# The reciprocal square root of the key norms moved from VectorE to GpSimd in a fused decoder layer

## What is computed

```python
q = jax.nn.elu(q) + 1.0
k = jax.nn.elu(k) + 1.0
k = k / jnp.sqrt(jnp.sum(k * k, axis=-1, keepdims=True) + EPS)    # EPS = 1e-6, over the 8 numbers of a head
scores = jnp.einsum('bhqd,bhkd->bhqk', q, k)
attn = jnp.einsum('bhqk,bhkd->bhqd', scores, v)
```

## Time and profile before

| | us |
|---|---|
| time, median of 2 runs | 458.34 |
| the two runs | 457.92 and 458.75 |
| span of the profiled execution | 457.6 |
| VectorE (DVE) busy | 384.1 |
| TensorE (PE) busy | 378.9 |
| GpSimd (POOL) busy | 296.1 |
| ScalarE (ACT) busy | 251.1 |

### The profile page before, as it was taken

The page is one execution under the profiler, slowest core; times in us unless marked ns, Lnnn a source line. Parts: engine busy times, 40 slices in busy tenths (PEclk is TensorE's granted clock), DMA queues, the critical chain, the costliest instruction groups (busy, mean ns, idle before and its releaser), DMA issues. The chain is left out here.

```text
span 457.6 us, 8365 instructions
## 1 busy us (share of the span) xinstructions
PE 378.9 (83%) x2057; PEld 263.5 (58%) x2057; DVE 384.1 (84%) x953; ACT 251.1 (55%) x483; POOL 296.1 (65%) x464
## 2 busy tenths in 40 slices
PE   3998878899898979898898989797989888977562
PEld 3776547657474746566565747484837475637242
DVE  2678885699999999999999989999999996956562
ACT  2646265565655555656565656666556554634232
POOL 1014586787777777787786858686867778554123
PEclk9999999999999999999999989999989998998756
DMA  8500000000000000000000000000000000000000
GB/s 235 107 13 1 13 1 13 7 6 11 3 12 13 11 11 0 23 0 23 0 23 0 23 0 23 0 23 0 23 0 23 0 12 2 11 2 11 1 11 23
DMA packets 13683, 8.20 MB, mean 18 GB/s; under 512 B 992, under 2 KB 13280, under 8 KB 13664
## 3 DMA queue, kind: packets, MB, share of 16 engines
q1 hardware_dynamic: 13376, 6.93, 5.6%
q10 hardware_dynamic: 288, 1.05, 0.7%
HBM read 5.88 MB, written 2.10 MB: 17 GB/s over the span
## 5 line engine op out<-in xcount | busy, mean ns | idle before, releaser
L1534 PE MATMUL S<-M,x1T 128*128 (+1 forms) x128 | 60.8, 597 | 0.0
L1574 PE MATMUL F<-w_gu,wT 128*128 128x352 f32 x128 | 48.5, 503 | 7.4 <-DVE h L1127 3.5
L472 POOL TENSOR_TENSOR xo_w<-pe 128x512 f32<-128x512 f32 x32 | 42.8, 1337 | 4.2 <-ACT pe L760 4.1
L1082 DVE TENSOR_REDUCE smax<-S 128x16 fp32r<-128x1024 f32 x32 | 39.1, 1221 | 5.4 <-DVE stats_post_attn L1049 2.8
L760 ACT ACTIVATE pe<-S 128x1024 f32<-128x1024 f32 x32 | 32.5, 1015 | 19.5 <-PE S L1542 19.5
L1542 PE MATMUL S<-smax,ident_r 128*128 128x512 f32 x64 | 24.0, 458 | 22.8 <-DVE smax L1082 22.7
L1574 PEld LDWEIGHTS F<-w_gu,wT 128*128 128x128 f32 x128 | 22.7, 197 | 33.5 <-DVE h L1127 14.0
L497 POOL TENSOR_TENSOR wT<-wT,hs 128x704 f32<-128x704 f32 x16 | 22.2, 1386 | 28.0 <-DVE wT L939 28.0
L460 POOL TENSOR_TENSOR kn<-fk,krn 128x256 f32<-128x256 f32 x16 | 11.1, 692 | 42.2 <-DVE krn L1038 42.2
L481 POOL TENSOR_TENSOR fw_v<-pe,srec 128x1024 f32<-128x1024 f32 x16 | 30.4, 1902 | 11.6 <-DVE srec L1094 11.6
L1524 PE MATMUL TP<-HW,ctx_cur 128*64 128x512 f32 x128 | 34.2, 660 | 0.0
(11 more groups left out here) (179 smaller groups left out, 1038.6 us busy)
## 6 DMA issues: line engine op xcount, KB each, us to landing
x_sb<-in_x SPq DMA_DIRECT2D x16, 128.0 KB, 2.1
out<-xv_w SPq DMA_DIRECT2D x16, 128.0 KB, 1.8
xk_w<-in_L_xattn_Wk ACTq DMA_DIRECT2D x1, 512.0 KB, 4.0
ctx_rows<-in_ctx SPq DMA_DIRECT2D x1, 512.0 KB, 6.9
xv_w<-in_L_xattn_Wv ACTq DMA_DIRECT2D x1, 512.0 KB, 6.6
xq_w<-in_L_xattn_Wq SPq DMA_DIRECT2D x1, 512.0 KB, 7.7
xo_w<-in_L_xattn_Wo SPq DMA_DIRECT2D x1, 512.0 KB, 9.4
fw<-in_L_ffn_w_gate SPq DMA_DIRECT2D x3, 64.0 KB, 4.2
```

What stands on the lines that cost most here:

```text
L472: ge.tensor_tensor(phalf[t].rearrange("p (h r) -> p h r", h=HX), p4[:, :, 0, :], p4[:, :, 1, :], ALU.add).then_inc(fold_made, 1)
L1082: ve.tensor_reduce(smax[:, t, :], S[:, :].rearrange("p (h r) -> p h r", h=HX), AX.X, ALU.max, negate=True).then_inc(smax_made, 1)
L1534: last = te.matmul(S[:, half * BANK:half * BANK + BANK], x1T[:, t * P:t * P + P], M[:, HC * half:HC * half + HC, bass.ds(b * R, R)], start ...
L1574: last = te.matmul(bk[:, 0:I], xfT[:, t * P:t * P + P], w_gu[:, m, :], start=True, stop=True)
```

## The change

The addition and the reciprocal square root become two instructions of GpSimd, ahead of k_norm: kse = kss + eps_attn, and krn = kse to the power neg_half, both on 128x32. The eleven operations leave VectorE. krn_step counts two steps per batch instead of eleven, and the tiles kyy and kxyy go.

```diff
@@ gpsimd
+            def k_rsqrt(b):
+                pool.wait_ge(kss_made, b + 1)
+                if late(b):
+                    pool.wait_ge(krn_step, 2 * b)
+                ge.tensor_tensor(kse[:, :], kss[:, :], eps_attn[:, :], ALU.add).then_inc(krn_step, 1)
+                pool.wait_ge(krn_step, 2 * b + 1)
+                if late(b):
+                    pool.wait_ge(kn_made, b)
+                ge.tensor_tensor(krn[:, :], kse[:, :], neg_half[:, :], ALU.pow).then_inc(krn_step, 1)
+
             def k_norm(b):
-                pool.wait_ge(krn_step, 11 * b + 11)
+                pool.wait_ge(krn_step, 2 * b + 2)
...
                 if b0 is not None:
+                    k_rsqrt(b0)
                     k_norm(b0)
@@ vector
             def k_sums(b):
                 dve.wait_ge(ksq_made, b + 1)
                 if late(b):
-                    dve.wait_ge(krn_step, 11 * b)
+                    dve.wait_ge(krn_step, 2 * b)
...
-            def k_rsqrt(b, first, last):
-                for k in range(first, last):
-                    if k:
-                        dve.wait_ge(krn_step, 11 * b + k)
-                    else:
-                        dve.wait_ge(kss_made, b + 1)
-                    if k == 0:
-                        ve.tensor_scalar(kse[:, :], kss[:, :], ATTN_EPS, None, ALU.add).then_inc(krn_step, 1)
-                    elif k == 1:
...
             def iteration(i):
                 b0, b1, b2, b3, b4, b5 = (on(i, n) for n in range(6))
-                if b1 is not None:
-                    k_rsqrt(b1, 4, 5)
...
-                    k_rsqrt(b1, 10, 11)
                 keep_units(i, {1: (11,)})
...
-                if b0 is not None:
-                    k_rsqrt(b0, 0, 1)
```

More of the change, by code:

```diff
@@ L58, in decoder_layer @@
     STEP = 2.0 ** 22
-    RSQRT_MAGIC = float(0x5F3759DF)
     HIGH_MASK = -(1 << 12)
@@ L130, in decoder_layer @@
         krn = sb("krn", [P, T * HA])
-        kyy = sb("kyy", [P, T * HA])
-        kxyy = sb("kxyy", [P, T * HA])
         kn = sb("kn", [P, T, P])
@@ L1259, in iteration @@
                     aggregate("ffn", b5)
-                if b0 is not None:
-                    k_rsqrt(b0, 0, 1)
                 keep_units(i, {0: (5,), 1: (25,)})
-                if b0 is not None:
-                    k_rsqrt(b0, 1, 2)
                 keep_units(i, {0: (7,)})
@@ L1268, in iteration @@
                 keep_units(i, {0: (9,)})
-                if b0 is not None:
-                    k_rsqrt(b0, 2, 3)
                 if b4 is not None:
                     gate_times(b4, 0)
-                if b0 is not None:
-                    k_rsqrt(b0, 3, 4)
                 if b4 is not None:
```

## The result

The changed kernel takes **541.74 us** (median of 2 runs, 540.59 to 542.88), the kernel before 458.34 us. The ratio is 1.181, with a 95% interval of 1.176 to 1.187: slower by 18%. The forecast was 558 us, with 478 to 596 as its range.

The account below looks back on a forecast made before the run. The prediction took the ring from kss through kvT to the next kss as the bound, not VectorE's busy time. 458.3 + 92.4 for the turns + 7.2 for the clock gave 558 us, range 478 to 596.

Parts of the forecast that it names:

- The ring: Path every turn goes round once, kss to kvT and on to the next kss: 23.65 us, setting the turn.
- The way from kss to kvT = 5.46 + X: From kss's end to kvT's start via GpSimd's addition, power and kn: 5.46 us plus X, against 6.79 before.
- X: Time of GpSimd's power on 128x32, forecast 7.5 us; break-even at 1.33, each microsecond moving the whole by 16 us.
- I put a tenth of it there: Pricing the power: 0.05 of the 499 ns by which it exceeds an addition is paid once, the rest by column.
- The clock: TensorE's granted clock falls in every steady turn after 7 us standing: 0.9 us in eight previously spared turns, 7.2 us.
- The sum: Eleven steady turns at 6.17 us, 67.9, plus the first five turns: 92.4 us; with the clock's 7.2, 557.9 us.
- GpSimd busy should rise by 124 us: Expected sign: GpSimd's added power and addition, 7.75 us in each of 16 turns, raise its busy time.
- VectorE's fall by up to 45: Expected sign: VectorE's busy time falls by up to 45 us as its eleven instructions leave.
- Columns partly overlapped: Rival: the power's column arithmetic overlaps, X 1.9 to 5 us; 491 us at X = 3.3, span 468 to 518; 27 in 100.
- A fixed amount: Rival: the power's extra cost is paid once per instruction, X 0.75 us; 449 us, span 448 to 467; 12 in 100.
- The clock stays down: Rival: standing keeps TensorE at 1.2 GHz all the turn, making it the bound; about 670 us; 3 in 100.
- has just room: GpSimd's queue from kvT on, with kn ending 0.8 us and not 1.7 us before kvT; no cost was added.

## Why the prediction was right, and where it was off

**The ring, not the busy time, decides: right.** The eleven instructions are gone from VectorE and the kernel is 18% slower. The power twice gave 15.7 us per us of power, against 16 forecast. Downwards, with half the columns, it was 22; that the clock's loss shrank with it is the likely reason and was not tried.

**The way from kss to kvT = 5.46 + X: right, with 0.2 us too little.** In the run with ten filling products, where the clock stays up over this stretch, kss ends at 250.99 and kvT starts at 262.14:

```profile
250.60 0.39 DVE L1022 TENSOR_REDUCE kss<-ksq 128x32 f32<-128x256 f32 x1
...
262.14 0.29 DVE L1029 TENSOR_TENSOR kvT<-A,head_mask 128x128 f32<-128x128 f32 x1 [5.01 <-PE A L1463]
...
278.82 0.39 DVE L1022 TENSOR_REDUCE kss<-ksq 128x32 f32<-128x256 f32 x1
```

That is 11.15 us, and 5.46 + 5.44 = 10.90. From kvT to the end of the next kss it is 17.07, against 16.85. Together 0.47 us more in a turn than the sum says. Of this, 0.19 stand ahead of the addition: it starts 3.79 us after the end of kss, not 3.60, and a small power ahead of it takes 0.98 us, where the row of before has 0.73.

```profile
251.03 0.98 POOL L518 TENSOR_TENSOR rstd_post_attn<-veps_post_attn,neg_half 128x2 f32<-128x2 f32 x1
```

Why it does, and where the rest falls, was not tried.

**X, the size of the power: off by 2.06 us (7.5 against 5.44).** The step that failed is "I put a tenth of it there": of the 499 ns by which a power on two columns exceeds an addition I gave 50 ns to what is paid once. It is 0.377 us before the first column, against 0.19 for an addition, so 0.18 of the 0.499 us are paid once, more than a third. Sixteen times the error: 33 us too much in the sum. Two columns cannot tell a slope from a fixed part; the slope per column then took up every error in the fixed part fifteen times.

**The clock: off by some 12 us the other way.** The step that failed is the count, not the price: "0.9 us in the eight that were spared: 7.2 us". In the ten loop turns the clock costs 8.6 us, 0.86 a turn, which is about that price. But a power stands in the first five turns too, where I had no term for the clock (7.7 us), and some 4.3 us lie behind the last kss. Taken together 20.6, of which the kernel before had 1.8 already (458.34 to 456.55): the change brought 18.8, against 7.2.

**The sum.** With X = 5.44 the prediction's terms give 458.3 + 14.2 for the first five turns + 11 x 4.11 + 7.2 = 524.9 us. With the gaps of both kernels filled, the changed one is 64.6 us longer, where these terms without the clock have 14.2 + 45.2 = 59.4. Up to the sixth kss it is 14.8 of the 64.6, and in the ten loop turns (420.05 - 137.66) - (359.32 - 122.88) = 45.95, where the terms have 41.1: that is the 0.47 a turn. Ring + 5.2 and clock + 11.6 lead to 541.7. So it was partly luck that 558 came within 16 us: the power was 33 us too dear and ring and clock 17 us too cheap. A forecast with the right power alone would have been 17 us too low.

**Busy time.** "GpSimd busy should rise by 124 us": it rose by 80.1, while power and addition alone are 91.1; GpSimd's other instructions got shorter (kn 628 ns in the mean, 692 in the earlier trace rows); that fewer of VectorE's stand beside them is the likely reason and was not tried. "VectorE's fall by up to 45": it fell by 54.3.

**The rivals.** *Columns partly overlapped* had its range (1.9 to 5 us) just below what came. 30 more columns did cost less than 15 times what two cost, but by the fixed part and not by its mechanism, a saving in longer rows: the power is linear from 2 to 32 columns. *A fixed amount* is false as well, but its price was measured: the multiplication in the power's place gives 451.05 us, where the rival had 449. It came close by another path than I named: a multiplication is cheaper than the 0.75 us that the rival had, and its fast turns still take 23.0 us, not 22.57, while four of the ten turns to the last kss take 24.6. *The clock stays down* all the turn: false, in the windows it is back at 1.00 some 7 us after it fell. What no rival had was the second bound under the ring, GpSimd's own queue: 505 us even with the power needed by nobody. The prediction had said of GpSimd only that it "has just room".

## What to carry to other kernels

Before work is moved to an engine with idle time, look at which wait it shortens and in whose queue it then stands: here eleven instructions of 0.26 us in the mean left a full engine, and one of 5.44 us entered the ring that every turn goes round, so each of its microseconds counted some 16 times when it was added, and 22 when half of it was taken away. Ask for a second size before an operation is priced from one short row, since a guess of the fixed part is multiplied by the columns. And where TensorE stands longer than before, ask twice: for the wait itself and for the products behind it, which may run at the lower clock, in the first and the last turns as well. It need not cost: in the kernel with ten filling products some turns still had a fall, and were no longer for it. Unused products in the gap show how much of the loss is the clock's, as long as they end before the wait does: ten of them gave 20.6 us back, twenty made the kernel slower.

## What was not expected of the hardware

- A power on GpSimd takes 0.377 us and 0.158 us for each column of 128 partitions, linear within a few ns over 2, 16 and 32 columns; an addition there takes 2.0 ns for each further column, so a column of power is worth some 79 columns of addition.
- The power runs at the same 5.44 us whether VectorE reads two SBUF inputs beside it or not, and does not hold VectorE up, while beside additions on 128x256 the same operations took 0.65 in place of 0.19 us, and beside the fold on 128x512 another small operation, of 0.19 us in the median, took 1.01.
- TensorE's clock falls even in the kernel before and in the faster versions, behind a wait of 1.79 us, in some turns and not in others (22.96 against 24.57 us with two Newton rounds). With three unused products of 1.46 us together it is 1.00 in every turn of the loop. What decides between the turns was not found.
